# Five shared-expert tiles as a ninth expert at the end of the middle stage, with the last stage's first normalisation inside them

## What is computed

```python
def _expert(x, w1, b1, w3, b3, w2, b2):
    h = jax.nn.silu((x @ w1 + b1) * (x @ w3 + b3))
    return h @ w2 + b2
...
    rw = jnp.zeros((T, E), dtype=xf.dtype).at[jnp.arange(T)[:, None], idx].add(w)   # two of E = 8 per token
    ...
    y = jnp.einsum('te,ted->td', rw, oe)
    z = _expert(xf, sw1, sb1, sw3, sb3, sw2, sb2)      # the shared expert
    return (y + z).reshape(shape)
```

## Time and profile before

| | us |
|---|---|
| median of 3 runs (1289.08 to 1292.20) | 1291.93 |
| the profiled execution | 1292.68 |
| its span | 1290.9 |
| stage 1 | 0 to 487 |
| stage 2 | 488 to 872 |
| stage 3 | 872 to the end |

### The profile page before, as it was taken

The page is one execution under the profiler, slowest core; times in us unless marked ns, Lnnn a source line. Parts: engine busy times, 40 slices in busy tenths (PEclk is TensorE's granted clock), DMA queues, the critical chain, the costliest instruction groups (busy, mean ns, idle before and its releaser), DMA issues. The chain is left out here.

```text
span 1290.9 us, 27101 instructions
## 1 busy us (share of the span) xinstructions
PE 1128.2 (87%) x8935; PEld 763.8 (59%) x8967; DVE 904.2 (70%) x2190; ACT 677.7 (52%) x1464; POOL 541.6 (42%) x729
## 2 busy tenths in 40 slices
PE   4688988889889885999999999971999999999998
PEld 2235555455455544998889888860556556556555
DVE  5687887778878835776666666652867867867865
ACT  2156555555555544666565666541554554554553
POOL 4342333323233227992222222215356456456424
PEclk9599999999999997999999999985999999999999
DMA  3427524334432204543332335433314413414302
GB/s 117 88 59 205 106 52 91 74 59 102 72 75 58 43 17 141 164 132 91 118 112 83 115 113 143 118 97 119 115 33 132 132 33 130 130 33 132 96 1 98
DMA packets 97179, 123.62 MB, mean 96 GB/s; under 512 B 14160, under 2 KB 86672, under 8 KB 96080
## 3 DMA queue, kind: packets, MB, share of 16 engines
q1 hardware_dynamic: 86288, 104.16, 30.0%
q0 software_dynamic: 6720, 18.36, 5.0%
q10 hardware_dynamic: 4096, 0.14, 0.2%
HBM read 83.26 MB, written 39.19 MB: 95 GB/s over the span
## 5 line engine op out<-in xcount | busy, mean ns | idle before, releaser
L458 ACT ACTIVATE p<-bank 128x384 f32<-128x384 f32 (+1 forms) x384 | 193.1, 528 | 197.0 <-PE bank L834 151.0
L668 DVE TENSOR_REDUCE neg_max<-bank 128x1 f16<-128x384 f32 (+3 forms) x352 | 218.7, 641 | 82.5 <-PE bank L822 71.9
L379 POOL TENSOR_SCALAR_AFFINE_SELECT p<-p 128x256 f32<-128x256 f32 x256 | 103.3, 407 | 262.2 <-ACT p L458 260.9
L113 PE MATMUL xbank<-gT_hi,w_hi 128*128 128x256 f16 (+1 forms) x636 | 174.9, 275 | 9.5 <-DVE w_lo L1261 5.8
L115 PE MATMUL xbank<-gT_hi,w_lo 128*128 128x256 f16 (+1 forms) x636 | 174.8, 275 | 0.0
L114 PE MATMUL xbank<-gT_lo,w_hi 128*128 128x256 f16 (+1 forms) x636 | 174.7, 275 | 0.0
L819 PE MATMUL bank<-k_stack,q_stack 96*128 96x384 f16 (+3 forms) x512 | 133.6, 313 | 40.6 <-DVE neg_max L668 29.7
L1165 POOL DMA_INDIRECT xg<-xn_dram,token_now x76 | 72.9, 959 | 196.5 <-PE xbank L1385 144.8
L1213 ACT ACTIVATE a<-xbank,b 128x256 f32<-128x256 f32 x159 | 74.3, 468 | 60.8 <-PE xbank L115 60.4
L834 PE MATMUL bank<-q_stack,k_stack 97*128 97x512 f16 (+1 forms) x256 | 91.3, 361 | 6.3 <-ACT p L458 3.5
L819 PEld LDWEIGHTS bank<-k_stack,q_stack 96*128 96x128 f16 x512 | 46.5, 99 | 80.5 <-DVE neg_max L668 58.3
(11 more groups left out here) (271 smaller groups left out, 3070.8 us busy)
## 6 DMA issues: line engine op xcount, KB each, us to landing
w_bc<-wT_dram SPq DMA_DIRECT2D x8, 2048.0 KB, 8.3
y_dram<-y SPq DMA_DIRECT2D x53, 256.0 KB
w<-in_w SPq DMA_DIRECT2D x11, 704.0 KB, 4.3
pack<-in_pack SPq DMA_DIRECT2D x14, 293.5 KB, 3.0
xr<-in_x SPq DMA_DIRECT2D x8, 512.0 KB, 7.0
xn_dram<-xn SPq DMA_DIRECT2D x8, 512.0 KB, 3.9
qk_hi_dram<-qk_hi SPq DMA_DIRECT2D x16, 256.0 KB, 2.1
qk_lo_dram<-qk_lo SPq DMA_DIRECT2D x16, 256.0 KB, 2.2
```

The source lines that it names most:

```text
L113: pe.matmul(out, hi_a(c), hi_b(c), start=first and x == 0, stop=False)
L379: pool.affine_select(out=diagonal, in_=diagonal, pattern=[[0, 2], [1, P]], compare_op=ALU.is_ge, fill=0.0, base=0, channel_multiplier=-1). ...
L458: act.activation(p32[:, s // GH % 2, s % GH, cols], s_bank[n][:, 0:cols.stop - cols.start], ACT.Exp).then_inc(p_exp.sem, 1)
L668: dve.tensor_reduce(neg_max[:, g % 2, 0:GH * TT].rearrange("p (h t) -> p h t", t=TT)[:, heads[0]:heads[-1] + 1, j], a_bank[c % 2][:, 0:len ...
```

## The change

- Of the 16 shared tiles, 11 (`HEAD_TILES`) stay at the start. The last 5 (`TAIL_TILES`) come after the routed tiles, as expert 9 with the shared weights: the two copies that nobody used are now copies of the shared expert. Their input rows are gathered through the same table, which gets 10 more columns and 10 more entries (`TAIL_PLACES`), so `table` has 74 matmuls of 110 columns instead of 64 of 100.
- The table is due after 9 tiles instead of 14. GpSimd makes all 64 `in_lane`, 16 `in_column` and the 10 new ones; VectorE makes 48 `in_column`, six in each of the first eight tiles (`place`), from a float16 copy of `lanes`.
- The weight pack is split in 12 parts instead of 14: ten in the head, two in the first two tail tiles.
- SyncE stores a routed tile's y in that tile's own turn and not in the next one's; so `new_expert` follows the store of the last tile of the expert before. The loads of the biases move into `new_expert`. The results of the routed experts go to a tensor of their own (`y_routed`).
- Step 0's front moves into the tail tiles (`Front` holds its buffers for both stages): `xin` and `ysh` are loaded at `new_expert(9)`; GpSimd's sum, its 8 gathers and the tail tiles' own gathers stand in one fixed order; VectorE adds rows at the ends of tail tiles 2 and 3 and within tile 4; the rest comes in `tail`.
- Stage 2 no longer ends with a wait for the last store; SyncE waits for it at the start of stage 3, after it has issued three small loads.

```diff
@@ over_experts
-            with eng.Fori(2, SHARED_TILES - AHEAD) as i:
-                tile(i, 0, 0, True)
+            for i in range(2, HEAD_TILES - AHEAD):
+                tile(i, 0, 0, HEAD)
             table()
...
-            tail(eng.value_load(bounds[0:1, E:E + 1], min_val=MIN_TILES, max_val=ROUTED_TILES) + (SHARED_TILES - 1), 0)
+            after = eng.value_load(bounds[0:1, E:E + 1], min_val=MIN_TILES, max_val=ROUTED_TILES) + HEAD_TILES
+            new_expert(E + 1, 1)
+            for t in range(TAIL_TILES):
+                tile(after + t, 1, min(t, 1), t)
+            tail(after + (TAIL_TILES - 1), 1)
@@ SyncE
             def new_expert(e, u):
                 if is_int(e, 0):
                     return
+                if is_int(e, E + 1):
+                    sp.wait_ge(y_stored.sem, y_stored.at(HEAD_TILES - 1))
+                    sp.dma_start(front.xin[:, :, :], token_rows(dram["x1"])).then_inc(front.xin_loaded.sem, 16)
+                    sp.dma_start(front.ysh[:, :, :], token_rows(dram["y"])).then_inc(front.xin_loaded.sem, 16)
+                    return
+                load_biases(e + 1, 1 - u)
...
+            def tile(i, u, before, stage, to_split=None):
+                if stage == ROUTED:
+                    store(i, dram["y_routed"], i - HEAD_TILES)
+                    return
+                if stage not in (HEAD, TURN):
+                    store(i, dram["y"], HEAD_TILES + stage)
+                    return
@@ GpSimd
+            gather(end + (HEAD_TILES + 1))
+            pool.wait_ge(front.xin_loaded.sem, front.xin_loaded.at(0))
+            pool.tensor_tensor(front.x2[:, 0, :, :], front.xin[:, :, :], front.ysh[:, :, :], ALU.add).then_inc(front.x2_base.sem, 1)
+            gather(end + (HEAD_TILES + 2))
+            pool.wait_ge(y_stored.sem, y_stored.at(end + (HEAD_TILES - 1)))
+            pool.wait_ge(front.slot_s.sem, front.slot_s.at(0))
+            pool.nop(nofuse=True)
+            gather_rows(0)
+            gather(end + (HEAD_TILES + 3))
+            gather_rows(1)
+            gather(end + (HEAD_TILES + 4))
+            gather_rows(2)
+            gather_rows(3)
+            pool.wait_ge(front.dve_ln.sem, front.dve_ln.at(0))
...
@@ VectorE
+                if stage == TAIL_TILES - 1:
+                    first_sums(3)
+                    first_statistics()
+                if has_next(stage):
+                    x_part(i + 1)
...
+                if stage == HEAD and i < PLACED_BY_DVE // PLACED_A_TILE:
+                    place(i)
+                if stage in (HEAD, TURN) and not is_int(i, 0):
+                    pack_part(i - 1)
+                elif stage in range(2):
+                    pack_part(HEAD_TILES - 1 + stage)
+                elif stage == 2:
+                    first_sums(0)
+                elif stage == 3:
+                    first_sums(1)
+                    first_sums(2)
...
+            def place(i):
+                if i == 0:
+                    dve.wait_ge(lanes_half_s.sem, lanes_half_s.at(0))
+                for n in range(PLACED_A_TILE * i, PLACED_A_TILE * (i + 1)):
+                    dve.tensor_scalar(in_column[:, n, :], lanes_half[:, 0:ROUTED_SLOTS // P], pos_f[:, 0, n // 2, n % 2:n % 2 + 1],
+                                      ids[:, n // 2:n // 2 + 1], ALU.is_equal, ALU.mult).then_inc(placed.sem, 1)
...
+            def first_sums(t):
+                dve.wait_ge(front.slot_s.sem, front.slot_s.at(0))
+                dve.wait_ge(front.x2_base.sem, front.x2_base.at(0))
+                dve.wait_ge(front.gathered[t].sem, front.gathered[t].at(0))
+                for k in range(2):
+                    if k:
+                        dve.wait_ge(row_sum.sem, 2 * t + 1)
+                    dve.scalar_tensor_tensor(front.x2[:, 0, t, :], front.rows_k[:, t, k, :], front.wk[:, t, k:k + 1], front.x2[:, 0, t, :],
+                                             ALU.mult, ALU.add).then_inc(row_sum.sem, 1)
+                dve.wait_ge(row_sum.sem, 2 * t + 2)
+                dve.bn_stats(front.stats[:, t, :], front.x2[:, 0, t, :]).then_inc(stats_s.sem, 1)
@@ TensorE
+            def tail(i, u):
+                out(i, u)
+                pe.wait_ge(front.xn_ready.sem, front.xn_ready.at(0))
+                for c in range(DC):
+                    for t in range(TT):
+                        mm = pe.transpose(front_bank[c][:, t * P:(t + 1) * P], front.xn[:, t, c * P:(c + 1) * P], identf[:, :])
+                    mm.then_inc(front.xT_psum.sem, 1)
@@ layer1_phase
-            pipeline(sp, front, step, store)
+            end = sp.value_load(route["bounds"][0:1, E:E + 1], min_val=MIN_TILES, max_val=ROUTED_TILES)
+            sp.wait_ge(front.tile_stored.sem, front.tile_stored.at(end + (SHARED_TILES - 1)))
+            sp.nop(nofuse=True)
+            pipeline(sp, step, store)
@@ weights
-        return np.concatenate([shared[None], routed, routed[-1:], routed[-1:]])
+        return np.concatenate([shared[None], routed, shared[None], shared[None]])
```

More of the change, by code:

```diff
@@ L50 @@
 SLOTS = (MAX_TILES + AHEAD) * ETOK
[L51 removed]
+TAIL_TILES = 5
+HEAD_TILES = SHARED_TILES - TAIL_TILES
+ROUTED_SLOTS = SLOTS + (TAIL_TILES - SHARED_TILES) * ETOK
+PLACES = 2 * T // P
+TAIL_PLACES = TAIL_TILES * ETOK // P
+PLACED_BY_DVE = 48
+PLACED_A_TILE = 6
+HEAD, TURN, ROUTED = "head", "turn", "routed"
 LAT, INTER, UP = 128, 128, 1024
@@ L1143, in tile, with last @@
                     load_weights(2, 0)
+                if is_int(i, HEAD_TILES - 1):
+                    load_pack(PACK_PARTS - 1)
+            def last(e, u, first):
+                if is_int(e, 0):
+                    store(HEAD_TILES - 1, dram["y"], HEAD_TILES - 1)
             def prologue():
@@ L1147, in prologue @@
                 load_weights(0, 0)
-                load_biases(0, 0, 0)
+                load_biases(0, 0)
                 load_x(1)
-            def tail(i, u):
-                store(i)
-                sp.wait_ge(y_stored.sem, y_stored.at(i))
-            over_experts(sp, prologue, new_expert, tile, after_first, lambda e, u, first: None, lambda: None, tail)
+            over_experts(sp, prologue, new_expert, tile, lambda e, u, first: None, last, lambda: None, lambda i, u: None)
             sp.nop(nofuse=True)
@@ L1252, in last @@
                 split_out(e + 1, 1 - u, first)
-            over_experts(act, prologue, new_expert, tile, after_first, last, lambda: None, lambda i, u: None)
+            over_experts(act, prologue, new_expert, tile, after_first, last, lambda: None, tail)
         @block.vector
@@ L1303, in total_y, with tile @@
                 ins.then_inc(y_ready.sem, 1)
-            def tile(i, u, before, ahead, to_split=None):
-                if not ahead:
+            def tile(i, u, before, stage, to_split=None):
+                if names_tokens(stage):
                     name_tokens(i + AHEAD)
@@ L1372, in table, with x_transposes @@
                 dve.wait_ge(tokens_s.sem, 1)
-            over_experts(dve, prologue, new_expert, tile, after_first, last, table, total_y)
+            over_experts(dve, prologue, new_expert, tile, after_first, last, table, tail)
         @block.tensor
         def _(pe):
-            def x_transposes(i, shared):
-                if shared:
+            def x_transposes(i, loaded):
+                if loaded:
                     pe.wait_ge(x_loaded.sem, x_loaded.at(i))
                 else:
-                    pe.wait_ge(gathered.sem, gathered.at(i - SHARED_TILES))
+                    pe.wait_ge(gathered.sem, gathered.at(i - HEAD_TILES))
                 for c in range(DC):
@@ L1591, in rows, with pipeline @@
             return t[bass.ds(b * S, S), :].rearrange("(t p) d -> p t d", p=P)
-        def pipeline(eng, front, step, tail):
-            front(0, 0)
+        def pipeline(eng, step, tail):
             step(0, 0, False, True)
@@ L1984, in step @@
                 dve.tensor_tensor(comb_lo[:, :], comb_bank[:, :], comb_hi[:, :], ALU.subtract).then_inc(comb_lo_s.sem, 1)
-            def first(b, u):
-                slots(b)
-                for k in range(2):
-                    sums(b, u, k)
-                statistics(b, u)
-                slots(b + 1)
-                x_low(b)
-            pipeline(dve, first, step, total_y)
+            pipeline(dve, step, total_y)
         @block.tensor
```

318 lines of the change are left out of this document (201 added, 117 removed).

## The result

| | median, us | runs | ratio to the kernel before |
|---|---|---|---|
| before | 1287.88 | 7 (1283.17 to 1292.2) | |
| after | 1302.61 | 7 (1295.22 to 1304.56) | 1.0103 [1.008, 1.0125] |

The change made the kernel 1.0% slower in these runs; 1278 was forecast, and the upper end of the range was 1293. (The same two kernels, run again twice, gave ratios of 0.9954 and 0.9999: see the experiments. None of the three is the forecast gain.) The profiled execution after took 1304.56, its span is 1302.8.

The account below looks back on a forecast made before the run. TensorE, busy 87% of the span, was taken to bound the kernel. Terms -29.2, -1.3, -1.0, +12.8, +2.4, +1.0, -3.0 and +3.7 sum to -14.6, giving 1278 us (range 1266 to 1293).

Parts of the forecast that it names:

- Weight loads one tile later: Expert switches: later weight loads leave TensorE waiting about 1 us instead of 1.4 to 2.3; -3.0 us, ends -8 and +10.
- the prediction's own sign of being wrong, over 3: Expert switches: TensorE waits over 3 us there would show the forecast wrong.
- collide worse: Rival at expert switches: biases, store and weights in a row delay the gather 1.5 us more; +13, 1294 us; chance 0.14.
- GpSimd waits in the tail: Tail tile 1: GpSimd's sum waits for `xin` and `ysh`, delaying the gather TensorE needs; +12.8 us, ends 10 and 15.
- Clock behind it: After the stall in tail tile 1: TensorE's clock is lost and returns late; +2.4 us, ends 0 and 4.
- Gathers of the front: Tail: step 0's 8 gathers stand between the tiles' own, thinly covered; +1.0 us, range 0 to 4.
- The seam: Between stages 2 and 3: of 39.0 us before stage 3's first product, 9.8 stay; -29.2 us.
- Step 0: Start of stage 3: part of the 2.3 us lost to half clock is regained; -1.3 us.
- longer seam: Rival between stages 2 and 3: new straight code, block end and clock cost +6, 1284 us; chance 0.12.
- The table: After nine head tiles: GpSimd's entries end 3.2 us after TensorE arrives, plus 0.5 for ten more matmuls; +3.7 us.
- VectorE in the head: Head tiles: six `place` operations a tile fit within 1.7 us of VectorE slack; 0 us.
- `place` held behind GpSimd: Rival in the head: each `place` waits for a GpSimd operation, +2.9 us in 8 tiles, 1298 us; chance 0.13.

Follow-up runs that it names:

- group 4: Kernels run on one chip: the kernel before again, 1318.8 us, the changed kernel again, 1318.7 us (ratio 0.9999), and two variants.
- e2: The kernel before with only the late weight load, behind the store of the last tile of the expert before: 1295.3 us, ratio 1.0078.
- e1: The changed kernel with weight loads back in their earlier place and no bound reads between store and load: 1276.6 us, ratio 0.9926.
- e4: The changed kernel with weight loads put back, no bound reads ahead of them, and `xin` and `ysh` loaded early: 1269.4 us, ratio 0.9863.
- e3: The changed kernel with `xin` and `ysh` loaded right behind the store of the head's last tile: 1287.9 us, ratio 1.0000.
- e14: The changed kernel with weights put back, base rows and three small loads early, 56 entries by VectorE, tail tile 3's gather earlier: 1289.9 us, ratio 0.9784.
- e11: The changed kernel with stage 3's three small loads (bias, corr, neg_bz) issued in the tail: 1309.2 us, ratio 0.9934.
- e5: The kernel before with SyncE's expert loop written out and the two bounds read ahead of the stores: 1276.5 us, ratio 0.9904.
- b0: The kernel before, unedited, run and profiled again: 1318.8 us, ratio 1.0000.
- e6: The changed kernel with weight loads in their earlier place and the two bound reads between store and load: 1282.1 us, ratio 0.9942.
- e9: The changed kernel with an expert's bias loads behind its weight loads instead of ahead: 1292.4 us, ratio 1.0029.
- e10: The changed kernel with the weight load held until the gather of the expert's second tile landed, bounds read ahead: 1324.7 us, ratio 1.006.
- e12: The changed kernel with the weight load held until the gather of the expert's third tile landed: 1328.5 us, ratio 1.0064.
- group 3: Kernels run on one chip beside the kernel before: the changed kernel again, 1312.4 us (ratio 0.9954), and three variants.
- groups 3 to 5: Three later sets of kernels, each run on one chip beside the kernel before; stage 3 took 414 to 417 us instead of 389 to 396.
- group 1: The first follow-up set, e1 to e4, run on one chip beside the kernel before: ratios 0.9926, 1.0078, 1.0000 and 0.9863.

## Why the prediction was wrong, step by step

- **Weight loads one tile later, -3.0: the step that failed.** It had the places right (biases, then weights, beside the gather of the expert's second tile) and the price wrong. It held that the load "keeps its length", that the gather "should end near 10" after the tile's start and be waited for by 1. The loads took 5.8 us to land in the median instead of 4.7, seven of the waits were 1.6 to 3.6 (the prediction's own sign of being wrong, over 3, came twice), and it left out the clock: 5.8 us of R to Z. In the first runs the stretch grew by 11.4, and the extra collision in the tail cost 2.87 and not 1 (851.15, the transposes for tail tile 1): 14.3 against -3.0, beyond the upper end given, +10. The rival "collide worse" (+13, 1294) named this; it got 0.14. This is 17 of the 26.5 us between the forecast (-14.6) and the profile (+11.9). In group 4 the stretch is -1.3 and the tail's wait 0.27, within the term's ends. Its size is thus not one number: the kernel before stood at the edge of the same collision. Why it was so large in the first runs stays open; e2 shows that the late load costs, by 0.8%.
- **GpSimd waits in the tail, +12.8: right.** 12.99, and 11.96 to 14.25 in the runs that kept it; the chain is the one forecast (store, loads, sum of 2.34, gather). Removing its cause gave less, 7.2 from e1 to e4, since other gathers come to be waited for. *Clock behind it, +2.4*: the next tile took 9.21 instead of 6.33, so 2.9.
- **Gathers of the front, +1.0:** 0 after, since the stall had given GpSimd the time; with the stall gone tail tile 3 waits 5.25 (e3) or 2.77 (e4) for its rows.
- **The seam, -29.2:** from the transposes of tail tile 4 (887.58) the first product comes 21.4 later; forecast 19.4. The chain up to `out` was right to 0.4 (901.26, by the terms 901.6); then `out` ran at half clock (3.4 instead of 2.0), the front's transposes and casts took 0.3 more, and the block's end and start 0.8 more. The rival "longer seam" was a third true.
- **The table, +3.7: too small.** The transposes around it are 16.62 apart instead of 9.84: +6.8. GpSimd was forecast well: its last entry starts at 559.9 and takes 0.74, so it ends at 560.7 (forecast 561), and 110 columns take 0.74 to 0.77. But TensorE was there at 556.3 and not at 557.8, so the wait is 4.56 and not 3.2; and the 74 products take 5.2 for the 3.5 forecast. Of this 0.3 is their width (110 columns; 3.87 at full clock in e14), the rest half clock behind the wait, which no term held.
- **Step 0, -1.3: the sign was wrong**, +4.9 in stage 3 (+2.2 in group 4). I had counted the late small load as harmless beside TensorE's products. But ScalarE's first sigmoid waits for it, 5.75 us behind the first product (914.77 to 909.02) and not 0.84 as in the kernel before, and everything of the router comes later. By then GpSimd is at the sum for step 1, and it holds VectorE's `chosen`; in the kernel before this sum had ended at 909.04, and `chosen` took 0.18 at 909.91 (there the sum held the operation ahead of it, `l_onehot`, 1.36 for the two instead of 0.29). Nor was the half clock shortened: it ended 6.4 us behind the first product (at 915.4), in the kernel before 4.4 behind it (at 906.3; the earlier trace rows give 4.4 too, and not the 4.8 of the prediction). Rows of the timelines, before and after:

```profile
902.80 0.20 ACT L1758 ACTIVATE l_sc<-ybank 128x32 f32<-128x32 f32 x1 [0.32 <-PE ybank L115]
...
907.84 1.36 DVE L1882 TENSOR_TENSOR l_onehot<-iota,l_topi 128x32 f32<-128x32 f32 x2
```

```profile
914.77 0.20 ACT L1947 ACTIVATE l_sc<-ybank 128x32 f32<-128x32 f32 x1
...
919.31 2.67 DVE L2072 TENSOR_TENSOR chosen<-l_onehot 128x32 f32<-128x32 f32 x1
...
919.57 2.35 POOL L1871 TENSOR_TENSOR x<-xin,ysh 128x1024 f32<-128x1024 f32 x1
```

  In e11, where the router is earlier than this sum, the same operation takes 0.21:

```profile
904.99 0.21 DVE L2073 TENSOR_TENSOR chosen<-l_onehot 128x32 f32<-128x32 f32 x1
```

- **VectorE in the head, 0: right.** The 48 operations take 302 ns in the median and 452 at most, beside a GpSimd without a gap, and the head tiles stay 6.33 apart. So the rival "`place` held behind GpSimd" (0.13) fell. The rows show the other direction: in seven of the eight tiles the GpSimd operation that runs when `place` ends and `pack_lo` follows takes 1.54 to 2.02 us instead of 0.6 or 0.74. The Trainium skill ("SBUF — State Buffer", Who interferes with whom) lets a `tensor_scalar` in a 2-port mode and a GpSimd operation block each other, the later one waiting for the whole of the earlier. None of the 48 waited so, and whether they ran in such a mode no row tells. Of an operation with two SBUF inputs the same section says that it contends with a GpSimd instruction that reads SBUF; `chosen`, a sum of two halves of one tile, agrees, 2.67 against 0.21.

The seam, the stall and the head came out within 2 us each. What decided was a term of 3 us in a loop with eight switches; without it the changed kernel would still have missed 1278 by some 9 us, by the table and step 0. In group 4, where the two kernels came out level, the forecast gain is missing too, with no single term to blame: the 11.5 us between -14.6 and -3.1 are spread over R to Z, step 0, the table, and the tail with the seam, 2.6 to 3.7 us each.

## What to carry to other kernels

Before a transfer is moved in a queue, look at what it will start beside, to the microsecond, and count that collision once per turn of the loop; the term of a step that is repeated needs a range of its own, also in the kernel before, whose place may be an accident. Where an engine waits a few microseconds in each turn, price the clock with the wait. And an experiment that rewrites a loop may move something small (here two register reads) that is worth about as much as what it undoes: compare the offsets in the trace before believing it. And a kernel that is to be compared should run again beside its variants: here its ratio went from 1.010 to 0.995 unedited.

## What the runs showed of the hardware

- A gather of 2 x 128 rows that starts level with a load of 1056 KB is used 5.7 us after the issue of its second half, or 7.3; with the load 1.5 ahead, within 3.8 (721.94 to 725.69). The weight load itself lands 4.6 us after its issue in the median when it is ahead (e1, e4, e5), 4.6 to 4.8 when it is level with no bias load right in front of it (before, b0, e6, e9), and 5.4 to 5.8 where the bias loads stand in front (after, e3, e10, e12). So what lengthens it goes with the bias loads in front, not with the gather beside it. The Trainium skill ("DMA: Bandwidth & Descriptors", Queues, rings and completion order) says that a DMA engine takes turns, packet by packet, between the queues that have work; that the gather is slower beside the load fits this, but no row shows the packets' order.
- Reading two loop bounds cost SyncE 1.6 us between a store and a load (2.37 less 0.82); without them ahead of the load the kernel before is 1.0% faster (e5).
- Stage 3 has two lengths for the same program. ScalarE's row of the first sigmoid of a step, of the changed kernel in the first runs and again in group 3:

```profile
963.00 0.20 ACT L1947 ACTIVATE l_sc<-ybank 128x32 f32<-128x32 f32 x1 [3.08 <-PE ybank L122]
```

```profile
952.64 0.20 ACT L1947 ACTIVATE l_sc<-ybank 128x32 f32<-128x32 f32 x1 [7.82 <-remote]
```

  It waits 4.7 us longer, for something that the profile does not name, in the second to the seventh of the eight steps, on three chips in groups 3 to 5; one of these chips ran group 1 without it. The cause stays open. So does why R to Z of one and the same kernel differs by up to 10 us between executions profiled in different groups.
